# Self and cross attention on one core: three staging places for projection weights, and softmax exponentials by group on ScalarE

## The reference

```python
xq = round_to_fp8(ln_out / in_scale)              # per feature, through bfloat16
q, qx = LN(xq @ wq.T), LN(xq @ wqx.T)             # 16 heads of 128
k, v  = LN(xq @ wk.T), xq @ wv.T                  # 8 groups of 128
core  = softmax(q @ k.T / sqrt(128)) @ v          # self attention, 64 keys
xout  = softmax(qx @ kx.T / sqrt(128)) @ vx       # cross attention, 1601 keys
cat   = concatenate([core, xout], axis=-1)
out   = round_to_fp8(cat / proj_smooth) @ wproj.T
```

## Time and profile before

| | |
|---|---|
| median of 3 runs | 2558.35 us (2553.39 to 2562.48) |
| profiled execution | 2558.61 us |
| its span | 2556.8 us |
| mean granted TensorE clock | 0.938 |
| busy: TensorE, VectorE, ScalarE, GpSimd | 89%, 76%, 61%, 55% of the span |

### The profile page before, as it was taken

The page is one execution under the profiler, slowest core; times in us unless marked ns, Lnnn a source line. Parts: engine busy times, 40 slices in busy tenths (PEclk is TensorE's granted clock), DMA queues, the critical chain, the costliest instruction groups (busy, mean ns, idle before and its releaser), DMA issues. The chain is left out here.

```text
span 2556.8 us, 49697 instructions
## 1 busy us (share of the span) xinstructions
PE 2265.1 (89%) x18258; PEld 1853.1 (72%) x18258; DVE 1937.0 (76%) x4407; ACT 1553.2 (61%) x3131; POOL 1408.7 (55%) x1558
## 2 busy tenths in 40 slices
PE   2767867999999999999999999999999999684666
PEld 1545656888888888888888888888888887462334
DVE  8989867777878777787777778777777877378753
ACT  5766655676776777677667767776776766211211
POOL 4343347766766677676667766676776676010000
PEclk8878879999999999999999999999999999896788
DMA  3112121111111111111111111101111010161100
GB/s 115 59 51 76 50 76 43 42 38 44 35 36 42 34 37 34 48 36 35 34 41 37 34 48 36 35 28 47 37 34 44 18 36 28 67 227 49 38 13 9
DMA packets 74671, 119.41 MB, mean 47 GB/s; under 512 B 21360, under 2 KB 56768, under 8 KB 73408
## 3 DMA queue, kind: packets, MB, share of 16 engines
q1 hardware_dynamic: 74432, 116.23, 13.5%
HBM read 94.20 MB, written 22.02 MB: 45 GB/s over the span
## 5 line engine op out<-in xcount | busy, mean ns | idle before, releaser
L75 PE MATMUL x_kc<-x_wk,x_ctxT 128*128 128x256 f16 x4992 | 623.4, 274 | 11.3 <-ACT x_sq L952 11.3
L75 PE MATMUL x_ox<-x_ctxp,x_pt 128*128 128x256 f16 x4992 | 611.5, 274 | 0.0
L75 PEld LDWEIGHTS x_kc<-x_wk,x_ctxT 128*128 128x128 f16 x4992 | 489.6, 98 | 82.8 <-ACT x_sq L952 14.5
L708 POOL TENSOR_SCALAR x_kT<-x_kf 128x512 f16<-128x512 f32 (+1 forms) x448 | 275.1, 614 | 473.2 <-ACT x_kf L960 472.9
L75 PEld LDWEIGHTS x_ox<-x_ctxp,x_pt 128*128 128x128 f16 x4992 | 485.4, 98 | 53.8
L710 POOL TENSOR_TENSOR x_kT<-x_kf,x_kT 128x512 f16<-128x512 f32 (+1 forms) x448 | 490.0, 1094 | 37.4
L1417 DVE TENSOR_TENSOR x_pt<-x_tp,x_pt 128x512 f16<-128x512 f32 (+1 forms) x512 | 288.7, 584 | 220.8 <-ACT x_pt L989 220.8
L1360 DVE TENSOR_REDUCE x_ss<-x_sq 128x4 f32<-128x512 f32 (+1 forms) x448 | 283.0, 643 | 170.1 <-ACT x_sq L952 169.4
L960 ACT ACTIVATE x_kf<-x_tp,x_hv 128x512 f32<-128x512 f32 (+1 forms) x448 | 331.8, 759 | 112.6 <-PE x_tp L1130 112.6
L948 ACT ACTIVATE x_kraw<-x_kc 128x512 f32<-128x512 f32 (+1 forms) x448 | 254.9, 569 | 150.7 <-PE x_kc L75 146.4
L989 ACT ACTIVATE x_pt<-x_tp 128x512 f16<-128x512 f32 (+1 forms) x512 | 259.3, 520 | 74.5 <-PE x_tp L1170 70.4
(11 more groups left out here) (253 smaller groups left out, 3062.5 us busy)
## 6 DMA issues: line engine op xcount, KB each, us to landing
x_stage<-in_ctxT SPq DMA_DIRECT2D x32, 800.5 KB, 4.4
x_stage<-in_ctx SPq DMA_DIRECT2D x16, 896.0 KB, 5.1
x_stage<-in_ctx SPq DMA_DIRECT2D x16, 640.0 KB
scr_q<-a_qxT SPq DMA_DIRECT2D x8, 1024.0 KB, 3.9
x_qs<-scr_q SPq DMA_DIRECT2D x16, 512.0 KB, 5.3
scr_core<-a_catc SPq DMA_DIRECT2D x8, 512.0 KB, 2.6
scr_x<-x_catx SPq DMA_DIRECT2D x8, 512.0 KB, 2.9
x_stage<-in_wprojT SPq DMA_DIRECT2D x16, 256.0 KB, 2.7
```

The lines of the kernel that those rows point to most:

```text
L75: last = pe.matmul(out, lhs[i], rhs[j], start=start and n == 0, stop=stop and n == len(parts) - 1)
L708: gp.tensor_scalar(dst[0], src, 1.0, 0.0, ALU.mult, ALU.add).then_inc(khi_ready, 1)
```

## The change

It does three things.

First, the projection weights get three staging places (the old one and two in `spare`, which nothing else uses until the block behind), each with its own semaphore; load n waits for the split of n - 3.

Second, in the self attention VectorE no longer subtracts the maximum. It multiplies it by minus the softmax scale, and ScalarE reads the scores from PSUM, one exponential per group of 64 columns with the maximum as its bias, and sums each into `sums` through its accumulator. VectorE's two sums fall away. The score banks are free only after their exponentials.

Third, the rounding of tile t's outputs moves: its three steps go into tile t + 1, between the negated maxima and the probabilities, and its sum behind the probabilities. keep_core(t) on GpSimd and store_core(t) on SP follow a tile later. Tile 6 still rounds its own at its end (after rounding tile 5's), tile 7 is rounded behind the tiles as before. The moments of banks 2 and 3 now stand behind the outputs.

```diff
-            sem_, value = {"s": (sub_ready, t * 2), ...
+            sem_, value = {"s": (exp_ready, t * 2), ...
...
-        wpst = flat[:, 3072:3584].rearrange("p (h n) -> p h n", n=C)
+        wpst = [w.rearrange("p (h n) -> p h n", n=C) for w in (flat[:, 3072:3584], spare[:, 0:512], spare[:, 512:1024])]
...
             for t in range(0, TILES - 1):
                 store_q(t + 1)
-                store_core(t)
+                if t:
+                    store_core(t - 1)
...
+            store_core(TILES - 2)
...
-                else:
-                    sp.wait_ge(wplo_ready, n)
-                sp.dma_start(wpst, ...).then_inc(wpst_ready, 16)
+                if n >= 3:
+                    sp.wait_ge(wplo_ready, n - 2)
+                sp.dma_start(wpst[n % 3], ...).then_inc(wpst_ready[n % 3], 16)
...
-            keep_core(0)
             for t in range(1, TILES - 1):
...
-                    gp.wait_ge(sub_ready, 2 * t + 2)
+                    gp.wait_ge(max_ready, 2 * t + 2)
...
-                keep_core(t)
+                keep_core(t - 1)
+            keep_core(TILES - 2)
...
             def exps(t, j):
-                act.wait_ge(sub_ready, t * 2 + j + 1)
-                act.activation(sm[:, 8 * j:8 * j + 8, :], sm[:, 8 * j:8 * j + 8, :], ACT.Exp,
-                               scale=SOFTMAX_SCALE).then_inc(exp_ready, 1)
+                act.wait_ge(max_ready, t * 2 + j + 1)
+                for i in range(8 * j, 8 * j + 8):
+                    src = tr[:, bank_of(("s", j)), (i - 8 * j) * S:(i - 8 * j + 1) * S]
+                    ins = act.activation(sm[:, i, :], src, ACT.Exp, bias=mx[:, i:i + 1], scale=SOFTMAX_SCALE,
+                                         accum_out=sums[:, i:i + 1])
+                ins.then_inc(exp_ready, 1)
...
-            def quantise(c, at, n, kept=None):
+            def rounding_steps(c, at, kept, count):
                 c.done(v.tensor_scalar(yb[:, at], ys[:, at], FP8_MAX, -FP8_MAX, ALU.min, ALU.max))
                 c.done(v.tensor_scalar(eb[:, at], yb[:, at].bitcast(U16), 0x7F80, None, ALU.bitwise_and))
+                if count:
+                    v.wait_ge(kept, count)
                 c.done(v.tensor_scalar(yf[:, at], eb[:, at].bitcast(BF16), FP8_MIN_NORMAL, FP8_ROUND, ALU.max, ALU.mult))
...
                     c.done(v.tensor_reduce(mx[:, 8 * j:8 * j + 8], src, X, ALU.max))
-                    v.tensor_tensor(sm[:, 8 * j:8 * j + 8, :], src, mx[...], ALU.subtract).then_inc(sub_ready, 1)
+                    v.tensor_scalar(mx[...], mx[...], -SOFTMAX_SCALE, None, ALU.mult).then_inc(max_ready, 1)
+                if 0 < t < TILES - 1:
+                    rounding_steps(c, slice(0, 2048), core_ready, t - 1)
...
                     v.wait_ge(exp_ready, t * 2 + j + 1)
-                    c.done(v.tensor_reduce(mx[...], e, X, ALU.add))
-                    c.done(v.reciprocal(mx[...], mx[...]))
+                    c.done(v.reciprocal(sums[...], sums[...]))
...
+                if 0 < t < TILES - 1:
+                    v.tensor_tensor(mg[:], yf[:], yb[:], ALU.add).then_inc(core_rounded, 1)
                 if t + 2 < TILES:
-                    moments(t + 2, range(4))
+                    moments(t + 2, range(2))
...
-                if not (isinstance(t, int) and t == 0):
-                    v.wait_ge(core_ready, t)
                 for j in range(4):
                     wait_filled(v, t, ("o", j))
...
-                if t < TILES - 1:
+                if t + 2 < TILES:
+                    moments(t + 2, range(2, 4))
+                if t == TILES - 2:
                     v.wait_ge(y_ready, t * 4 + 4)
-                    quantise(c, 0, 2048).then_inc(core_rounded, 1)
+                    rounding_steps(c, slice(0, 2048), core_ready, t)
+                    v.tensor_tensor(mg[:], yf[:], yb[:], ALU.add).then_inc(core_rounded, 1)
```

52 lines of the change are left out of this document (22 added, 30 removed).

## The result

The changed kernel takes 2544.29 us (median of nine runs, 2543.16 to 2548.85) against 2557.06 us for the kernel before, measured beside it: ratio 0.9952, 95% interval 0.9942 to 0.9961. That is 12.8 us faster by the medians and 12.3 by the ratio, where 2560 (2547 to 2573) was forecast and "faster" had a chance of 0.15. The prediction was wrong.

What follows compares the result with a forecast made beforehand. VectorE was taken to bound the self attention, with ScalarE and TensorE's chain deciding after the change. Tile 0 −2.4, five tiles +4.9, tiles 6 and 7 +6.9, projections −7.5 sum to +1.9 us: 2560 us, range 2547 to 2573.

Steps and rivals of the forecast that it cites:

- So today VectorE sets the period.: Self attention, kernel before: VectorE, with hardly a gap, bounds the 35.8 us tile; ScalarE is close behind.
- Part 3, the walk: Steady self-attention tile, followed engine by engine: the chain over ScalarE and TensorE decides, period 37.0 us instead of 35.8.
- the group of exponential: ScalarE's 64-column exponential with accumulator read: 0.34 us each, 5.4 us for 16 a tile; bounds 0.30 and 0.59.
- all behind it moves as it stands today: Steady tile: TensorE's second half of the probabilities comes 2.65 us later, and what follows keeps its present durations.
- The 1.4 for GpSimd beside VectorE and the 1.2 for the low clock: Added to the five tiles: 0.7 in each of two tiles for GpSimd's contention, 1.2 in one for TensorE's clock.
- Rival C: TensorE does probabilities, projections and transpositions on low clock in every tile, 1.2 us more in four further tiles: 2569, chance 0.17.
- Rival A: VectorE stays the bound, the exponentials hide, and 2.7 us a tile is gained in five tiles: 2532, chance 0.12.
- The page that was set aside: Trainium skill page: estimate of 0.20 us per 64-column exponential from PSUM, against 0.24 in the row preferred; advises against small tiles.
- Tile 0: First self-attention tile: loses its rounding and sum, pays for later outputs and moments, gains from uncontended centring; −2.4 us.
- Tiles 6 and 7: Last self-attention tiles: exponentials delay ScalarE's key units, so the first transposed key comes 6.9 us later, bounds +5 and +14.
- Projections: Last cross-attention tile: with three staging places GpSimd no longer waits for projection weight loads, 7.5 us gained over four steps.
- rival D: GpSimd's waits for the projection loads return as waits for ScalarE's keys, gain 1 instead of 7.5 us: 2567, chance 0.08.

Runs made afterwards that it cites:

- before_raw_ahead: Kernel before, with only TensorE's projections of the third and fourth next-tile units moved ahead of the third query unit, into the wait for the exponentials: ratio 0.9955.
- halved_exps: Changed kernel with each group's exponential split into two of 32 columns, only the second summed: ratio 1.0006 to the kernel before, 13.8 us slower than the changed kernel.
- filler: Changed kernel with TensorE repeating a next-tile projection six times in its wait for the exponentials, same result rewritten: ratio 0.9978 to the kernel before.
- turn_filler: Changed kernel with TensorE's repeated projection in its wait and ScalarE's third and fourth query units ahead of its two raw units: ratio 0.9932 to the kernel before.

## Why the prediction was wrong

**"So today VectorE sets the period."** This was only half right. It rested on VectorE's rows with "hardly a gap: 2.83 us ahead of the moments of bank 2". VectorE's work does fill all but 3.0 of the 35.76 us, but that gap is the part that can grow and shrink: it is ScalarE's copy behind TensorE's projections, which took 2.60 us in tile 1 and 3.01 in tile 2 where 1.89 is their time at full clock. before_raw_ahead shows 34.1 us for the same work of VectorE, with 1.78 of gap. The sum doesn't hang on this step, but the habit behind it, to take TensorE's durations as given, is the second term below.

**Part 3, the walk.** The chain was right: query units, probabilities, outputs, third units, statistics, with ScalarE idle 2.86 us ahead of its third units and 4.60 ahead of the normalisation (4.5 was forecast), and VectorE idle 1.85 ahead of the outputs. halved_exps confirms it: 2.3 us more of exponentials, 2.2 to 2.5 us more of tile. A period under 35.5 was to show "the walk over unit 2 is wrong"; the period was 35.4, but it was the durations in the walk that were wrong and not its way. **This is the step that failed**: two terms of the walk were mis-sized, and both were durations carried over from rows of the kernel before:
- the group of exponential, 0.34 us forecast with a lower bound of 0.30, measured 0.29 (0.20 to the read, 0.09 to the next). The second transposition comes 15.30 us behind the normalisation's start (167.80) instead of 16.06: 0.76.
- "all behind it moves as it stands today" carried the low clock of tile 1 along: from the second transposition to VectorE's outputs 6.15 us before (149.28 to 155.43), 4.86 after (183.10 to 187.96): 1.29. All of it lies in the two rows, 0.57 in the transposition (1.94 to 1.33) and 0.72 in the projections (2.60 to 1.89).

Together 2.05; the undisturbed tile took 35.06 instead of 37.0. Five times 1.94 is 9.7 of the miss of 10.7 us (+4.9 forecast, −5.8 measured).

**The 1.4 for GpSimd beside VectorE and the 1.2 for the low clock.** In place of these 2.6 us the trace has 0.5 in tile 1 and 1.06 in tile 3, all clock, the last 1.0 of the miss. GpSimd did slow VectorE in tile 2 (the third rounding step took 1.31 us, in tile 1 0.70), but VectorE had room there, and the tile was the shortest of the five. These are the rows that are longer there than 1.33 and 1.89 (tiles 1, 3, 3):

```profile
147.53 1.84 PE L1091 MATMUL a_tr<-a_ident,a_pp 128*128 128x128 f32 x8 [0.33 <-ACT a_qxf L878]
...
218.17 1.97 PE L1091 MATMUL a_tr<-a_ident,a_pp 128*128 128x128 f32 x8 [0.33 <-ACT a_qxf L878]
219.93 2.31 PE L75 MATMUL a_pr<-a_wp,a_xq 128*128 128x512 f16 x8
```

**Rival C** had the right resource and the wrong sign: TensorE's longer wait was to bring the low clock onto the critical work in every tile; the spell came to lie in the wait and on the rows ahead of the second transposition. Its sign, a clock of 0.5 throughout the second quarter of the tiles, nearly came true (0.5 from 176.4 to 183.2 of a quarter from 176.6 to 185.3), and would have misled: what counts is which rows lie in that time. **Rival A** (VectorE the bound, outputs not moved, 2532) fell: VectorE idles 1.85 us ahead of the outputs, and halved_exps moves the tile.

**The page that was set aside.** The exponential of 64 columns from PSUM took 0.20 us to its read. The estimate of 0.20 from the Trainium skill ("VectorE: DVE Perf Modes", section "The TRN2 errata") was met; the row preferred to it read from SBUF. The same section's advice against small tiles is borne out for the engine itself, since ScalarE spends 4.63 us on them where the two large exponentials and their waits took 2.05. It is not borne out for the kernel, which is faster with them (0.9952 against 0.9979). With 0.29 a group the forecast would have been 5 to 6 us lower, some 4 us under the kernel before and still inside "same"; most of the rest of the miss is the clock.

**Tile 0**: −2.4 forecast, −3.6 measured. **Tiles 6 and 7**: +6.9 forecast, +9.3 measured; with the cheaper groups the forecast would have been 5.3. The collision of keep_core of tile 5 with the rounding of tile 6 (2.64 and 2.49 against 1.09 and 0.69 in the kernel before, 3.4 us of the remaining 4.0) was missed: "two keep_cores follow each other" was looked at for its wait and not for what runs beside them. **Projections**: −7.5 forecast, −8.0 measured, right, and rival D fell.

In all the two traces differ by −10.1 us where +1.9 was forecast: −1.2 of this miss lies in tile 0, −10.7 in the five tiles, +2.4 in tiles 6 and 7, −0.5 in the projections, and −2.0 behind them, where the sum had nothing and the cause is open.

The chances failed with the walk. No case let TensorE's critical work get shorter: the lowest that the forecast's own bounds give is 2552 (−5 for the group, −3 for the clock), rival A stood at 2532, and nothing between them had a mechanism, where 2544 came out. The stated lower bound of 2547 was itself lower than these terms give.

## What to carry to other kernels

An engine without gaps is the bound only if the few gaps that it has are explained: look at what ends them, at which clock that work ran, and what it would take at full clock. A low spell of TensorE costs what the rows in it lose, and nothing where TensorE waits anyway, so an edit that moves a wait can move a price; a walk that carries durations over "as they stand" should give every TensorE row at both levels. Two parts of a change may each be worth nothing or less and still gain together, so try them as a square. Before a large rewrite try the order of the lists: moving two projections into TensorE's wait was worth as much as this whole change.

## What was not expected of the hardware

- Filling TensorE's longest wait with useless work made the kernel 6.6 us slower (filler), and with two units of ScalarE in another order 5.1 us faster (turn_filler). In filler the granted clock fell within TensorE's work, not in a wait.
- A small exponential from PSUM with a per-partition bias and its accumulator read follow each other at 0.29 us for 64 columns; with both exponentials of a group at 32 columns and one read, 16 groups took 6.90 us, 0.43 each (halved_exps). The durations printed in these rows grow from 0.30 to 0.36 us over a run of sixteen while the starts stay 0.29 apart: the starts are what counts.
- Runs of the changed kernel differ by 4 us, and with them the granted clock (0.941 against 0.943 to 0.945): a third of the gain that was to be measured.
- VectorE's rounding steps (bf16, one tensor operand) took 2.64 and 2.49 us beside GpSimd's two-operand subtraction (keep_core), 0.69 alone.
- The same program of tile 0 took 42.85 us in one trace and 44.43 in another, all of the difference from the clock of two groups of TensorE rows (the second transposition and the projections behind it).
